# A unit's decays made by one VectorE scan over broadcast rows, instead of by TensorE products, an exponential and GpSimd steps

## The reference, cut to what matters

```
g = -jnp.exp(A_log) * jax.nn.softplus(x @ Wa.T + dt_bias)
def step(state, inp):
    q_t, k_t, v_t, g_t, b_t = inp
    state = state * jnp.exp(g_t)[..., None, None]
    corr = jnp.einsum('bhk,bhkv->bhv', k_t, state)
    v_new = (v_t - corr) * b_t[..., None]
    state = state + jnp.einsum('bhk,bhv->bhkv', k_t, v_new)
    o_t = jnp.einsum('bhk,bhkv->bhv', q_t, state)
    return (state, o_t)
```

## Time and profile before

| | |
|---|---|
| median of 3 executions | 1167.6 us (1165.88 to 1169.84) |
| span of the profiled execution | 1164.1 us |
| around the span (median less span) | 3.5 us |
| TensorE busy | 1114.7 us (96%) |
| VectorE busy | 821.3 us (71%) |
| ScalarE busy | 703.5 us (60%) |
| GpSimd busy | 501.4 us (43%) |
| mean granted TensorE clock | 0.991 of full |

### The profile page before, as it was taken

How to read it: one execution, slowest core, us unless ns; L and a number is a source line. 1 busy time by engine, 2 the same in 40 slices (tenths; PEclk the granted TensorE clock), 3 DMA queues, 4 the chain that set the end, 5 groups by cost and what they waited for, 6 DMA issues and landing times.

```text
span 1164.1 us, 28733 instructions
## 1 busy us (share of the span) xinstructions
PE 1114.7 (96%) x11460; PEld 768.8 (66%) x11460; DVE 821.3 (71%) x1452; ACT 703.5 (60%) x1215; POOL 501.4 (43%) x709
## 2 busy tenths in 40 slices
PE   8989799999999999999997899889999999999998
PEld 3444455555555555565554556679999899989987
DVE  5989668868868778778767665676566666565562
ACT  5767477667677676776775866645444444444443
POOL 1659475685684783883975812212000000011000
PEclk9999799999999999999999999999999999999999
DMA  4222234545545555565555642252222221111100
GB/s 124 61 54 69 69 55 78 98 98 73 117 80 75 109 82 94 103 121 123 120 84 145 190 133 75 44 175 49 52 51 52 69 52 47 47 46 48 30 20 10
DMA packets 147284, 93.74 MB, mean 81 GB/s; under 512 B 80688, under 2 KB 130736, under 8 KB 146256
## 3 DMA queue, kind: packets, MB, share of 16 engines
q1 hardware_dynamic: 146000, 91.71, 35.8%
q10 hardware_dynamic: 1152, 0.21, 0.1%
HBM read 54.77 MB, written 14.55 MB: 60 GB/s over the span
## 4 chain that ended last, share of the span: by engine, by line
PE 76%; DVE 10%; POOL 5%; ACT 4%; issue 3%; SPq 1%; DMA 1%; ACTq 0%; DVEq 0%; POOLq 0%
PE proj L535 21%; PE out L1673 5%; PE gram L550 5%; PE turned_v_chain L1673 5%; PE proj L1735 4%; PE turned_v_chain L1747 4%; DVE conv L1143 4%; PE proj L1612 4%; PE gram L1647 2%; PE turned_v_chain L541 2%; PE out L559 2%; POOL inverse L1378 2%; PE decays L566 2%; POOL rank_one L1375 2%; PE turned_v_chain L684 2%
## 5 line engine op out<-in xcount | busy, mean ns | idle before, releaser
L1143 DVE SCALAR_TENSOR_TENSOR conv<-proj,kq_weights,conv 128x504 f32<-128x504 f32 (+2 forms) x261 | 189.8, 732 | 25.8 <-ACT conv L865 19.3
L535 PE MATMUL proj<-xT,vg_weights 128*128 128x512 f32 x384 | 189.8, 618 | 4.8 <-DVE conv L1143 2.0
L1990 POOL TENSOR_TENSOR rope<-rope_part,rope_part 128x512 f32<-128x512 f32 x32 | 42.1, 1336 | 321.5 <-DVE rope_part L1921 321.5
L535 PE MATMUL proj<-xT,kq_weights 128*128 128x512 f32 x348 | 168.7, 610 | 5.4 <-DVE conv L1143 5.1
L1143 DVE SCALAR_TENSOR_TENSOR conv<-proj,vg_weights,conv 128x504 f32<-128x504 f32 (+2 forms) x192 | 140.6, 733 | 39.3 <-ACT conv L865 34.3
L1378 POOL TENSOR_TENSOR inverse<-inverse,rank_one 128x30 f32<-128x30 f32 (+14 forms) x240 | 125.5, 523 | 18.8
L1375 POOL TENSOR_TENSOR rank_one<-inverse 128x30 f32<-128x30 f32 (+14 forms) x240 | 117.2, 488 | 22.2 <-DVE inverse L1187 7.3
L535 PEld LDWEIGHTS proj<-xT,kq_weights 128*128 128x128 f32 x348 | 62.4, 190 | 80.8 <-issue 69.4
L535 PEld LDWEIGHTS proj<-xT,vg_weights 128*128 128x128 f32 x384 | 68.4, 192 | 69.2 <-issue 61.3
L550 PEld LDWEIGHTS gram<-keys_q 128*64 128x64 f32 x896 | 56.8, 136 | 42.5 <-issue 24.9
L865 ACT ACTIVATE conv<-proj,kq_weights 128x512 f32<-128x512 f32 x87 | 59.6, 685 | 41.3 <-PE proj L535 40.9
(11 more groups left out here) (263 smaller groups left out, 2471.8 us busy)
## 6 DMA issues: line engine op xcount, KB each, us to landing
kq_weights<-in_kq_w SPq DMA_DIRECT2D x32, 390.0 KB, 6.9
vg_weights<-in_vg_w SPq DMA_DIRECT2D x32, 390.0 KB, 6.2
o_scratch<-oT SPq DMA_DIRECT2D x32, 256.0 KB, 2.2
o_in<-o_scratch SPq DMA_DIRECT2D x16, 512.0 KB, 4.0
o_rs<-o_rs_quarters SPq DMA_DIRECT2D x88, 64.0 KB, 5.9
diagonal<-gram_decayed SPq DMA_DIRECT2D x128, 32.0 KB, 1.9
inverse<-inverse SPq DMA_DIRECT2D x32, 128.0 KB, 2.8
q_first<-rope SPq DMA_DIRECT2D x128, 32.0 KB, 1.9
```

The costliest lines, as they stand in the source:

```text
L535: mm = e.matmul(bank(c, u)[:], w[:, (k * 3 + c % 3) * 128:(k * 3 + c % 3 + 1) * 128], xT[g][:, k, :], start=(k == 0), stop=(k == KD - 1))
L1143: e.scalar_tensor_tensor(acc(c, u)[:, :, back:], src[:, :, 0:S - back], weights(c, u)[:, j:j + 1], acc(c, u)[:, :, back:], ALU.mult, ALU.a ...
L1990: e.tensor_tensor(turned[half][:].rearrange("p b r q -> p r b q"), parts[2 * half][:], parts[2 * half + 1][:], op).then_inc(s_turned, 1)
```

## The change

The products of two factors become one recurrence along the tokens. Each unit's decay matrix has, in row p (a key step) and column l (a token), the product of the decays of the tokens after p up to l. VectorE makes a whole unit in one instruction: state = state * token_decay + begin, over 8 sequences x 64 tokens, where `token_decay` holds exp(g) of each token (the same in all 64 rows of a half, 0 at a sequence's start) and `begin` holds a 1 where the column is the row's own token. Such a matrix is causal already, so GpSimd's masked copy goes, and EE serves both products. For the lower left block (rows 64 to 127, first 32 tokens) which the solve needs too, `begin` carries the product of decays up to token 31, and GpSimd multiplies half a tile by a factor per row (`decay_low`).

The rows come from two small sets of TensorE products (`decay_rows`, one in slot 1 for units 0 to 7, one in slot 6 for the rest) and small exponentials (`exp_rows`). SyncE stores them to DRAM (`store_rows`) and loads them back for each unit, broadcast over 64 partitions (`load_decay`: three DMAs a unit, one buffer for all units, so it waits for the scan of the unit before). ScalarE no longer switches its table in slots 1 to 5 and 7 to 9, and computes one small exponential (`beta`) before slot 1 instead of in slot 2. VectorE gets two small memsets at the start, and `solve_load` writes its transposes to consecutive columns of `X` instead of strided ones.

```diff
-                def decays(u):
-                    e.wait_ge(s_steps, u + 1)
-                    wait(e, s_ee, u)
-                    wait(e, s_whiout, u - LAG + 1)
-                    e.matmul(EB[:], between_l[:], flat(steps), start=True, stop=True).then_inc(s_between, 1)
+                def decay_rows(part):
+                    if part == 0:
+                        e.wait_ge(d_const, 32)
+                        e.wait_ge(s_gdve, 15)
+                        e.wait_ge(s_z, 2)
+                        e.wait_ge(s_beta, 2)
+                    else:
+                        e.wait_ge(s_gpool, POOL_STEPS)
+                        e.wait_ge(s_rows, ROWS_DONE[0])
+                    for lo, hi, at in ROWS[part]:
+                        e.matmul(EB[0:hi - lo, at:at + ROW], decay[:, lo:hi], pick, start=True, stop=True)
+                    lo, hi, at = SINCE[part]
+                    e.matmul(EB[:, at:at + hi - lo], since_lhs, decay[:, lo:hi], start=True, stop=True).then_inc(s_rowmm, 1)
...
-                def exp_between(u):
-                    e.wait_ge(s_between, u + 1)
-                    wait(e, s_gm, 4 * (u - 1))
-                    wait(e, s_eem, u - 1)
-                    e.activation(flat(EE[u % 2]), EB[:], ACT.Exp).then_inc(s_ee, 1)
+                def exp_rows(part):
+                    e.wait_ge(s_row0, 2)
+                    e.wait_ge(s_rowmm, part + 1)
+                    for i, (lo, hi, at) in enumerate(ROWS[part]):
+                        for c in (slice(1, S), slice(S + S // 2 + 1, ROW)):
+                            e.activation(rows_of[part + i][0:hi - lo, c], EB[0:hi - lo, at + c.start:at + c.stop], ACT.Exp).then_inc(s_rows, 1)
+                    lo, hi, at = SINCE[part]
+                    e.activation(since[:, lo:hi], EB[:, at:at + hi - lo], ACT.Exp).then_inc(s_rows, 1)
...
+                def load_decay(u):
+                    e.wait_ge(d_rows, 48 if u < H else 144)
+                    wait(e, s_scan, u)
+                    some = slice(u * GB, (u + 1) * GB)
+                    for n, p in (("decay_first", slice(0, 64)), ("decay_second", slice(64, 128))):
+                        e.dma_start(token_decay[p, :], scratch[n][some, :].rearrange("b l -> (b l)")[None, :]
+                                    .broadcast_to([64, GB * S])).then_inc(d_token, 16)
+                    e.dma_start(begin[64:128, :].rearrange("p (b l) -> p b l", l=S)[:, :, 0:S // 2],
+                                scratch["decay_low"][some, :][None, :, :].broadcast_to([64, GB, S // 2])).then_inc(d_token, 16)
...
                 for s in range(SLOTS):
                     ua, ub, uc, uo = s, s - 1, s - LAG, s - LAG - 2
+                    if live(ua) and s > 0:
+                        load_decay(ua)
...
+                    if s == 0:
+                        e.dma_start(begin[:], a["begin"]).then_inc(d_begin, 16)
+                        e.wait_ge(d_begin, 16)
+                        store_rows(0)
+                        load_decay(0)
+                    if s == ROWS_SLOT:
+                        store_rows(1)
...
                     e.wait_ge(s_gram, 2 * u + r + 1)
                     if r == 0:
-                        e.wait_ge(s_ee, u + 1)
+                        e.wait_ge(s_low, u + 1)
                         wait(e, s_slo, u - LAG + 1)
...
-                    e.tensor_tensor(four(M[u % LAG], r), gram[:, :, 0:S], four(eem(u), r), ALU.mult).then_inc(s_gm, 1)
+                    e.tensor_tensor(four(M[u % LAG], r), gram[:, :, 0:S], four(EE[u % 2], r), ALU.mult).then_inc(s_gm, 1)
+
+                def scan_decay(u):
+                    e.wait_ge(d_token, 48 * (u + 1))
+                    wait(e, s_low, u - 1)
+                    e.tensor_tensor_scan(flat(EE[u % 2]), token_decay[:], begin[:], 0.0, ALU.mult, ALU.add).then_inc(s_scan, 1)
...
                     if turning is not None and live(ud) and s > U:
                         add_q_squares(ud)
+                    if live(ua):
+                        scan_decay(ua)
                     if s == LAG:
                         solve_scale_columns(0)
...
-                def decayed_causal(u):
...
-                def decay_steps(u):
-                    wait(e, s_between, u)
-                    e.tensor_tensor(steps[:], by_unit(decay[:])[:, group(u), head(u), :, None].broadcast_to([128, GB, S]),
-                                    between_r[:, None, :].broadcast_to([128, GB, S]), ALU.mult).then_inc(s_steps, 1)
+                def decay_low(u):
+                    e.wait_ge(s_scan, u + 1)
+                    e.wait_ge(s_rows, ROWS_DONE[0 if u < H else 1])
+                    half = EE[u % 2][:, :, 0:S // 2]
+                    some = slice(u * GB, (u + 1) * GB)
+                    e.tensor_tensor(half, half, since[:, some, None].broadcast_to([128, GB, S // 2]), ALU.mult).then_inc(s_low, 1)
```

More of the change, by code:

```diff
@@ L119 @@
 U = NG * H
+ROW = 2 * S + S // 2
 NS = 4
@@ L228, in delta_phase @@
         beta = flat(Y)
-        eem = lambda u: Wk if u == LAG - 1 else EEM
+        Vn4 = flat(Vn).rearrange("p (i c) -> p i c", i=4)
+        rows_of = [Vn4[:, i, 0:ROW] for i in range(3)]
+        pick, since_lhs = Vn4[:, 3, 0:ROW], gate[0][:, 0:2, :].rearrange("p b l -> p (b l)")
         VB, CH = flat(VC[:, 0:2, :]), flat(VC[:, 2:4, :])
@@ L255, in delta_phase @@
         s_silu = [sem(f"silu_{n}") for n in ("k0", "k1", "q", "v0", "v1", "g")]
-        s_steps, s_between, s_ee, s_eem = sem("steps"), sem("between"), sem("ee"), sem("eem")
+        s_row0, s_rowmm, s_rows, s_scan, s_low = (sem(n) for n in ("rows_begin", "rows_product", "rows", "decay_scan", "decay_low"))
+        d_begin, d_rows, d_token = sem("d_begin"), sem("d_rows"), sem("d_token_decay")
         s_gram, s_gm = sem("gram_kq"), sem("gram_kq_decayed")
@@ L426, in gate_weights, with store_rows @@
                         e.dma_start(scales[f"w_{n}"][:], a[f"{n}_scale"]).then_inc(d_gate, 16)
+                def store_rows(part):
+                    e.wait_ge(s_row0, 2)
+                    e.wait_ge(s_rows, ROWS_DONE[part])
+                    some = ((0, 0, GB * H),) if part == 0 else ((1, GB * H, 3 * GB * H), (2, 3 * GB * H, 4 * GB * H))
+                    for i, lo, hi in some:
+                        for n, c in (("decay_first", slice(0, S)), ("decay_second", slice(S, 2 * S)), ("decay_low", slice(2 * S, ROW))):
+                            e.dma_start(scratch[n][lo:hi, :], rows_of[i][0:hi - lo, c]).then_inc(d_rows, 16)
+                def load_decay(u):
[7 more added lines that the diff above has]
+                                scratch["decay_low"][some, :][None, :, :].broadcast_to([64, GB, S // 2])).then_inc(d_token, 16)
                 e.dma_start(w_ab[:], a["w_ab"]).then_inc(d_wab, 16)
@@ L696, in chain_low @@
                     mm.then_inc(s_wlo, 1)
-                decays(LAG - 1)
                 e.wait_ge(d_wc[0], 16)
@@ L919, in scalar @@
                 for tile, n, done in ((ident, "ident", d_ident), (dt, "dt_bias", d_small), (rate, "A_log", d_small),
-                                      (even, "even", d_small), (odd, "odd", d_small), (between_r, "between_r", d_const),
-                                      (between_l, "between_l", d_const), (causal, "causal", d_const)):
+                                      (even, "even", d_small), (odd, "odd", d_small)):
                     e.dma_start(tile[:], a[n]).then_inc(done, 16)
+                for part, n in ((pick, "pick"), (since_lhs, "since_lhs")):
+                    e.dma_start(part, a[n]).then_inc(d_const, 16)
                 e.preload_act_table_set(LN_EXP)
@@ L976, in scalar @@
                 tap(V0, 0)
-                e.preload_act_table_set(LN_EXP)
-                exp_between(last)
                 tap(V1, 0)
@@ L1496, in delta_phase @@
     tiles["ints"], tiles["scales"] = ints, scales
-    done = {"o": s_og, "w_high": s_whiout, "scaled": s_gr, "stored": d_out, "weights": d_w, "first": d_first, "uvo": d_uvo, "ffn": s_wgt, "up": d_up, "down": d_down, "scales": d_gate, "decays": s_ee,
+    done = {"o": s_og, "w_high": s_whiout, "scaled": s_gr, "stored": d_out, "weights": d_w, "first": d_first, "uvo": d_uvo, "ffn": s_wgt, "up": d_up, "down": d_down, "scales": d_gate,
             "gram": s_gm, "gate": s_silu[G], "v1": s_conv[V1], "high": s_wlo, "low": s_wloout, "solve": s_solve}
@@ L1601, in out @@
                         e.wait_ge(done["weights"], 16 * 12)
-                        e.wait_ge(done["decays"], U)
                         e.wait_ge(done["w_high"], U - NS)
@@ L2009, in shape_constants @@
     u = np.arange(S)
-    between_l = np.where(key[:, None] == 0, token[:, None] <= token[None, :], token[:, None] > token[None, :]).astype(f)
-    between_r = np.where(key[:, None] == 0, token[:, None] > u[None, :], token[:, None] <= u[None, :]).astype(f)
-    causal = (u[None, :] >= token[:, None]).astype(f)
+    first = key == 0
+    own = first[:, None] & (token[:, None] == u[None, :])
```

(4 more changed lines are left out.)

86 lines of the change are left out of this document (36 added, 50 removed).

## The result

The change made the kernel slower: 1206.5 us (median of 4 executions, 1201.6 to 1207.1) against 1167.6; the ratio is 1.0333, with a 95% interval of 1.0307 to 1.0359. The forecast had the direction, but 1188 us for the time and 1200 for the end of its range. The profiled execution has a span of 1204.6 us, 40.5 more than before (the medians are 38.9 apart: they lie 3.5 us above the span before and 1.9 with the change), where the forecast had 20.3. Sums from here on are made on the spans.

A forecast was written before the change was run, and what follows sets the result against it. VectorE was taken to pace the run-in and TensorE, narrowly, slots with the chain; +10.1 us for slots 11 to 32 and +10.2 for the run-in on a 1164.1 span gave 1184.4, a median of 1188, range 1173 to 1200.

The forecast's parts named there:

- The price of a scan: VectorE's scan of 512 columns: taken as 1.15 us, between 0.69 and 3.5; rival at half rate, 1.38, chance 0.22.
- Turning seams: At 5 seams behind turning slots the scan lies on the chain V1 waits for: 5 x 1.15 = +5.75 us.
- Loading seams: At 5 seams behind loading slots: 1.09 us waiting for GpSimd plus 1.15 scan, less 0.39 slack; 5 x 1.84 = +9.2.
- TensorE's product: Slots 11 to 32: losing the 0.96 us decays product gains only plain seams' slack, 4.9 us, not 21.1.
- The run-in: Before the steady slots: first units' longer way and scans on VectorE's path, less shorter waits and decays records: +10.2 us.
- TensorE loses the wide product: Slots 11 to 32: the decays product of 0.96 us a unit goes, gaining 4.9 us at the 12 plain seams.
- The end: From slot 33 on: nothing changes, no cost forecast.
- SyncE's queue: Rival: loads ahead of the weights make TensorE wait 0.5 to 1 us in 22 slots, 1199 to 1210 us; chance 0.10.

The follow-up runs named there:

- e4: Changed kernel with the scans of units 10 to 31 cut to 2 columns instead of 512, loads and all else kept: 1180.45 us, ratio 1.0131.
- e7: Kernel before the change, with TensorE's decays product of units 10 to 31 cut to 2 of 512 columns: 1159.69 us, ratio 0.9957.
- e6: Changed kernel plus two idle 128 x 512 products in TensorE's waits at seams behind turning and loading slots: 1187.54 us, ratio 1.0184.
- e5: Kernel of e1, with the scans of units 2 to 9 cut to 2 columns instead of 512: 1167.28 us, ratio 1.0015.
- e1: Changed kernel with the scan moved, from slot 10 on, off the seam to behind the slot's first decayed product: 1173.97 us, ratio 1.0083.
- e3: Changed kernel plus an unread 128 x 512 product per unit, slots 10 to 32, where the decays product stood: 1195.95 us, ratio 1.0271.
- e10: Changed kernel with each unit's three loads moved behind o_rs and both weight loads in SyncE's queue: 1202.89 us, ratio 1.0316.
- e11: Kernel of e8 with its first scan behind slot 9's inverse work and loads issued a slot earlier, behind the weights: 1161.38 us, ratio 0.9968.
- e8: Changed kernel with units 0 to 8 decayed the old way and units 9 to 31 scanned at the place of e1: 1168.26 us, ratio 1.0023.
- e2: Changed kernel with the scan moved behind the first decayed product in the 5 loading slots only: 1183.18 us, ratio 1.0153.

## Why the prediction was wrong, point by point

- **The price of a scan**, 1.15 taken between 0.70 and 3.5: right. The shortest record is 1.148 us. The Trainium skill's page named in the prediction ("DVE: opcode table, instruction layouts, handler registers and perf-mode slots", section 6) says half throughput. By e4 a scanned column costs 1.98 ns. VectorE's two products of gram and decays take 0.68 us for 512 columns and 0.42 for 256 (L1156 and L1162 of the kernel before), which makes some 1.04 ns a column as an estimate (one input of these products is the gram, and the scan reads `token_decay` and `begin`); a scanned column takes 1.9 times as long, and the trace agrees with the page. The prediction's estimate of 2 x 0.69 = 1.38 was too high, as it doubled the fixed part too (0.13 us of the scan's 1.148).
- **Turning seams**, +1.15 each: about right. From the V1 before to the one behind the turning slot it was 369.28 - 347.75 = 21.53 us, and is 389.92 - 367.37 = 22.55, so +1.02:

```profile
367.37 1.98 PE L568 MATMUL proj<-xT,vg_weights 128*128 128x512 f32 x4 [0.31 <-DVE conv L1179]
```

  (That V1's own wait rose by 1.15, from 0.37 to 1.52, proves nothing: TensorE also lost the 0.96 of the decays, and waits 0.66 for Y besides.)
- **Loading seams**, +1.84 each, with 1.09 of it waiting for GpSimd: right. V1 came 412.81 - 389.92 = 22.89 us after the one before it, and 390.36 - 369.28 = 21.08 before, so +1.81; e4 shows the waiting alone, 1.04.
- **TensorE's product**, worth 4.9 and not 21: right. With the slack of the loading seams (5 x 0.39) the forecast makes 6.85, and e7 measured 6.2 by the spans. Without half clock (e6) slots 11 to 32 cost 10.25 us, and the forecast had 10.1.
- **The run-in**, +10.2: the sum is right (10.7), and so are its first terms, but the agreement of the sum is in part luck:

```profile
35.58 1.23 DVE L1202 TENSOR_TENSOR_SCAN decayed<-token_decay,begin 128x512 f32<-128x512 f32 x1 [0.25 <-DMA begin<-decay_low_scratch]
37.60 0.69 DVE L1192 TENSOR_TENSOR gram_decayed<-gram,decayed 128x512 f32<-128x512 f32 x1 [0.80 <-POOL decayed L1459]
...
41.12 1.23 DVE L1202 TENSOR_TENSOR_SCAN decayed<-token_decay,begin 128x512 f32<-128x512 f32 x1 [1.56 <-DMA begin<-decay_low_scratch]
```

  The first decayed product stands at 37.60, as forecast, and the second scan waits 1.56 where 1.3 was forecast. The gain at ScalarE's waits was smaller: 4.0 fell to 2.5, not to 1.7. The eight later scans cost 7.0 (e5), where the forecast had 9.2 + 1.4 - 1.15 - 0.8 = 8.65 with the 1.4 allowed for GpSimd in the way; everything else cost 3.8, where it had 3.2 + 2.45 - 2.3 - 1.8 = 1.55. The two errors nearly cancel.
- **The step that failed** is a term that the sum did not have: "TensorE loses the wide product" and "Turning seams" were priced at full clock, although the same sum makes TensorE wait longer at ten seams (2.2 us at a turning and 2.5 at a loading one, as measured). Nine stretches at half clock followed, 15.3 us by their length and 14.1 by e6. The Trainium skill, "TensorE: Matmul & The Clock Gate" (HAM oscillation), says that waits (there for DMA) within a kernel can put the clock back to half; the trace agrees, by the 0.50 to 0.59 of the windows above, and the prediction should have made a rival of it. The row at hand was in the kernel before: the decays record of 1.22 us for one instruction at the end of the run-in the earlier trace rows, where two take 1.12 in a steady slot, and a granted clock of 0.50 over it. The prediction took 1.8 us off for these records without asking whether its own new waits would bring them elsewhere.
- **The end**, forecast at nothing, costs 5.4 us. TensorE waits longer for weights in slot 33, 4.24 us against 1.71 before:

```profile
651.08 2.91 PE L568 MATMUL proj<-xT,vg_weights 128*128 128x512 f32 x4 [4.24 <-DMA vg_weights<-in_vg_w]
653.91 1.07 PE L673 MATMUL turned_v_chain<-inverse,gram_decayed 32*32 32x32 f32 x32
```

  Its products after that wait are at half clock (2.91 us for four), and that is not the only place. The same two steps of a later slot, first before and then with the change:

```profile
668.99 1.15 PE L559 MATMUL out<-W_scaled,V 128*64 128x64 f32 x32 [1.64 <-POOL W_scaled L1467]
...
671.08 1.98 PE L535 MATMUL proj<-xT,vg_weights 128*128 128x512 f32 x4
```

```profile
706.31 1.75 PE L592 MATMUL out<-W_scaled,V 128*64 128x64 f32 x32 [1.64 <-POOL W_scaled L1499]
...
709.84 3.76 PE L568 MATMUL proj<-xT,vg_weights 128*128 128x512 f32 x4
```

  The wait is the same, and the clock behind it is not. From slot 33 to the last microseconds the changed kernel has four stretches of half clock (from about 651.8, 669.0 and, two in a row, 706.7), the kernel before has one (from about 629.6). Over the profiles of this case the end goes with their number, and hardly with the wait for weights. With one stretch it took 560.7 to 563.2 us (before, e1, e3, e4, e7, e10, e11), though those waits came to between 1.0 and 3.9 us; with two or three 564.1 to 564.5 (e8, e5, e2); with four 565.1 (e6) and 567.4 (the changed kernel). So most of the 5.4 is read as half clock too; no run fills these waits to show it. Why the clock fell behind one wait of 1.64 us and not behind the other, and what made the weights late, is not settled.
- **The rivals.** SyncE's queue reached the measured time (1199 to 1210), but is not what happened: in slots 11 to 32 no wait for weights ended a seam (TensorE waited for them once, 0.86 us at 276.11), and e10 gained about 0.17%. A range that took in the whole of that rival would have held the time, but for a wrong reason.

## What to carry to other kernels

Work taken from the bounding engine is worth only the slack up to the next chain at each wait; count seams of each kind, not units. When a change opens waits of some 2 us in TensorE's stream, add a term for the clock, and test it by filling the wait with idle products: if the kernel gets faster by doing more, it was the clock. An operation whose result is needed only later in the slot need not stand on the seam: moving the scan took off 33 of the 40 us, and going back to the old way in the run-in (with the loads behind the weights) another 13, 10.5 of them ahead of slot 10.

## What the runs showed that had not been expected

- A two-input VectorE instruction of 2 columns takes 0.14 us alone and 1.18 behind a GpSimd product under way (e4); the reverse holds GpSimd's 30 columns for 1.05 us instead of 0.25.
- Twenty-three products more made the kernel 0.6% faster (e3), and ten pairs of them in the waits 1.4% (e6).
- The same wait of 1.52 us behind a turning slot was followed by half clock at 211.07, 478.31 and 569.87, and not at 301.63 and 389.92. Over the runs it followed more often where TensorE had waited longer: 5 of 5 seams with 0.92 + 1.61 us, 3 of 5 with 0.66 + 1.52 (2 of 5 in e2), 3 of 5 with 1.61 alone (e3), 1 of 5 with 1.54 alone (e4), none of 5 with 1.3 alone (e1). What decides within a kind the runs don't show.
- The time of the changed kernel moves with its clock: three executions with a mean granted clock of 0.968 to 0.969 took 1206.5 to 1207.1 us, the fourth, at 0.977, took 1201.6.
